# A two-layer decoder: layer two's negated row maxima as bf16 parts, one unread product per sequence, and newly written queues

## The chip, the cores and the metric

The kernel is written for one Trainium2 chip and runs on one of its cores. Its engines work side by side, each down its own queue: TensorE (PE), VectorE (DVE), ScalarE (ACT), GpSimd (POOL) and SyncE (SP, which here only issues DMAs). They wait for each other on semaphores. The metric is device time in microseconds, the median of several executions; lower is better.

## The reference, cut to what matters

Sixteen sequences of 128 tokens with width 128 pass through two layers, every step fp32 and followed by a layer norm of x plus the step:

```python
# layer 1
x = ln(x + attention_with_relative_positions(x))      # 16 heads of 8
x = ln(x + cross_attention(x, ctx))                   # 16 heads of 64, 77 keys
x = ln(x + moe(x))                                    # 7 experts and a no-op, top 2, capacity 256
# layer 2
x = ln(x + ln_affine(x + linear_attention(x)))        # 16 heads, rank 16, decay and gate
x = ln(x + cross_attention(x, ctx))                   # 16 heads of 8, 77 keys
x = ln(x + bit_linear(silu(conv3(bit_linear(x)))))    # int8 activations, ternary weights
```

In layer two's cross attention, softmax needs each row's maximum over its 77 keys. The kernel forms exp(k q - max) with the keys on the partitions, so the maxima have to reach the products' accumulators transposed.

## The kernel before, in words

One tile is one sequence (128 tokens on the partitions, or width on the partitions after a transposition). Layer one is software-pipelined over the sequences t: prefix `a_` is self attention, `b_` cross attention, `rel*` the relative scores, `keys`, `v0` the context's projections, `r_*` the router's work in four batches of sequences (0 to 7, 8 to 12, 13 and 14, 15), `r_send` the scatter of tokens to expert slots. After all sixteen come the experts' products (`m_*`), and then layer two, again pipelined: `c_` gathers and norms the experts' output, `d_` is the linear attention, `e_` the cross attention, `f_` the convolutional feed-forward.

Each engine's queue is written out by hand. `ORDER1` and `ORDER2` hold one list of names per engine. `rounds` (L162) repeats the list for i = -8, -7, ...; an entry `name:s` emits that step for t = i + s. `TAIL1` ends layer one with entries `name:t`, skipping what has been emitted already; `UNTIL1` says where it takes over. An engine never passes over a step, so a step that waits holds all that is listed behind it on its engine. Below, `b_lg:14` is step b_lg for t = 14.

One round of layer two, by the steps that matter here. DVE masks the four groups of linear attention scores (d_m0 to d_m3, L1679), bounds f's exponential (f_clamp, L1771), does f_silu and f's quantization (f_q0 to f_q4, L1721 to L1752), sums and norms c, d (d_add, d_st, d_ag, d_n0, d_n1, D_st, D_ag, d_norm) and e (e_div L1323, e_add, e_st, e_ag, e_norm), turns the rotary products (d_r0, d_r1 L1657, d_rope L1663), quantizes f's input (f_i0 to f_i4), norms f's output (f_norm L1348), forms d's queries and keys (d_q L1667, d_k L1673), and takes e's four maxima (e_m0 to e_m3, L1363).

PE runs d_rank (L882, products of the rotary result), f_x (a transposition, L978), e_s (e's scores, which need ACT's copy qe of e_q), f_up (one bf16 and three fp32 products of 512 columns: six records), e_nm, d_s01 (the first three groups of d's scores), e_st (e's scores again, keys on the partitions), d_s3, e_inj, d_v, d_out, e_v. In e_nm, PE transposes the tile of negated maxima, ACT copies it to `nmT`, and e_inj (L714) adds row a of each 32-row strip (a from 0 to 3) to the accumulators of e_st: sixteen fp32 products with a selecting matrix `picksel`, four strips at once. Then ACT takes the exponentials e_e0 to e_e3. ACT also copies d_v's result to `xTr` (step d_v of its list, L1106), which d_out multiplies by the output weight; the sum d_add follows on DVE. In the trace an fp32 product makes two records, a bf16 one makes one. `idle(b, n)` issues n products of ones that nobody reads; before the change they stand at the start and end of layer two and near the end of layer one.

## Time and profile before

| | us |
|---|---|
| median of 3 runs (745.8 to 747.18) | 746.79 |
| the profiled execution | 751.72 |
| its span, first to last instruction | 749.9 |
| PE, DVE, ACT, POOL busy in the span | 664.9, 562.7, 420.0, 207.4 |

Layer one's rounds fill about 50 to 375, the routing's end and the experts 375 to 440, layer two's rounds the rest. Busy time says how much of a stretch an engine has instructions under way; which engine sets the pace of a stretch is read from who waits for whom. A name such as `k` or `bank` stands for several tiles, and buffer numbers are left out.

### The profile page before, as it was taken

How to read it: one execution, taken by the hardware profiler on the slowest of the kernel's cores; microseconds unless marked ns; L12 is line 12 of the kernel's file. 1: busy time of each engine (PE TensorE's matmuls, PEld its weight loads, DVE VectorE, ACT ScalarE, POOL GpSimd, SP SyncE). 2: the span in 40 equal slices, each digit the busy share in tenths (PEclk: the TensorE clock that was granted, in tenths of full speed). 3: DMA queues.
4: the chain of work that ended last, by engine and by line, in shares of the span. 5: the costliest groups of instructions: out<-in, count | busy, mean ns of one | idle time of the engine just before them, and what ended most of it. 6: DMA issues, size and time to landing. Idle time of an engine off the chain costs nothing.

```text
span 749.9 us, 20658 instructions
## 1 busy us (share of the span) xinstructions
PE 664.9 (89%) x7838; PEld 505.8 (67%) x7838; DVE 562.7 (75%) x2029; ACT 420.0 (56%) x1412; POOL 207.4 (28%) x213
## 2 busy tenths in 40 slices
PE   5877999999999999998878988999899989999896
PEld 2445677777777777776757976666666666666664
DVE  1246788888888999977656657888877888888853
ACT  3767777777777757763211224555555555555542
POOL 4411333333333335224434122222222222222100
PEclk9967999999999999999899999999999999999999
DMA  9775555555555435720122100000000001110000
GB/s 347 261 245 183 174 173 173 172 173 173 173 172 169 144 98 176 275 106 23 32 89 68 41 24 9 12 13 12 13 13 16 13 13 14 14 13 13 6 5 7
DMA packets 48257, 72.17 MB, mean 96 GB/s; under 512 B 2832, under 2 KB 43280, under 8 KB 45472
## 3 DMA queue, kind: packets, MB, share of 16 engines
q1 hardware_dynamic: 45120, 61.80, 24.4%
q0 software_dynamic: 2320, 5.18, 3.2%
q10 hardware_dynamic: 720, 3.88, 1.3%
q8 instruction: 63, 1.03, 0.6%
q14 instruction: 34, 0.28, 0.1%
HBM read 32.38 MB, written 38.47 MB: 94 GB/s over the span
## 4 chain that ended last, share of the span: by engine, by line
PE 49%; DVE 27%; ACT 12%; issue 8%; another core or an unknown queue 2%; DMA 2%; POOL 1%; SPq 0%; DVEq 0%; ACTq 0%
PE bank L562 40%; ACT sc L1072 4%; PE bank L623 4%; PE bank L710 3%; DVE k L1679 3%; DVE sc L1301 2%; DVE scol L1721 2%; ACT kbd L1221 1%; ACT kbd L1222 1%; ACT q L1111 1%; DVE k L1657 1%; DVE kbd L1771 1%; DVE nmxb L1370 1%; DMA xT_ld<-xT 1%
## 5 line engine op out<-in xcount | busy, mean ns | idle before, releaser
L1072 ACT ACTIVATE sc<-sc,nmxa 128x128 f32<-128x128 f32 x256 | 99.0, 391 | 37.2 <-DVE nmxa L1301 37.2
L501 POOL TENSOR_TENSOR early<-early,recb 128x616 f32<-128x616 f32 x32 | 38.9, 1216 | 179.5 <-DVE recb L1394 179.5
L1301 DVE CUSTOM_DVE_ANT_0 sc<-bank,rel 128x128 f32<-128x128 f32 x256 | 56.3, 286 | 14.7 <-PE bank L562 14.5
L1679 DVE TENSOR_TENSOR k<-bank,k_sb 128x512 f32<-128x512 f32 x64 | 41.1, 685 | 28.9 <-PE bank L562 22.2
L1072 ACT ACTIVATION_READ_ACCUMULATOR sc<-sc,nmxa 128x1 f32 x256 | 48.8, 191 | 0.0
L478 POOL TENSOR_TENSOR rext<-rext,ones 128x1008 f32<-128x1008 f32 x16 | 29.9, 1868 | 54.0 <-ACT rext L1050 53.9
L1050 ACT ACTIVATE rext<-bank 128x512 f32<-128x512 f32 x64 | 34.8, 610 | 17.6 <-PE bank L562 17.6
L623 PE MATMUL bank<-k_sb,sc 128*128 128x128 f32 x256 | 37.5, 294 | 7.3 <-issue 6.5
L562 PE MATMUL bank<-k,xdT 128*128 128x512 f32 x96 | 43.8, 592 | 0.0
L537 POOL TENSOR_TENSOR oTb<-x_all,row_sb 128x128 f32<-128x128 f32 x16 | 7.3, 458 | 131.8 <-DVE pTa L1700 131.8
L1311 DVE COPY pTa<-bank 128x512 f32<-128x512 f32 x32 | 21.2, 663 | 25.2 <-PE bank L623 25.2
L623 PEld LDWEIGHTS bank<-k_sb,sc 128*128 128x128 f32 x256 | 31.1, 151 | 11.9 <-issue 11.1
L562 PEld LDWEIGHTS bank<-xTb,wb 128*128 128x128 f32 x256 | 29.8, 191 | 12.5 <-issue 12.5
L510 POOL DMA_INDIRECT xg_dram<-x_all,to_slot x32 | 31.4, 980 | 24.7 <-DVE to_slot L1530 16.7
L527 POOL DMA_INDIRECT pTa<-yg_dram,of_slot x32 | 31.4, 980 | 24.6 <-DMA yg_dram<-sc 17.7
L1124 ACT ACTIVATE early<-early 128x308 f32<-128x308 f32 x64 | 27.5, 456 | 18.3 <-DVE early L1379 18.2
L562 PE MATMUL bank<-pTb,v 77*32 77x128 f32 x1024 | 33.9, 283 | 2.7 <-DVE early L1379 2.5
L562 PE MATMUL bank<-kbd 32*128 32x256 f32 x256 | 36.2, 400 | 0.1
L1116 ACT ACTIVATE pTb<-bank 77x512 f32<-77x512 f32 x64 | 34.2, 586 | 3.4 <-PE bank L562 3.4
L562 PE MATMUL bank<-k_sb,ones 128*128 128x256 f32 x144 | 36.0, 399 | 0.0
L562 PE MATMUL bank<-k,q 64*128 64x77 f32 x512 | 32.5, 276 | 2.2 <-ACT q L1111 1.6
L562 PEld LDWEIGHTS bank<-k,q 64*128 64x128 f32 x512 | 30.0, 187 | 6.4 <-ACT q L1111 5.9
(278 smaller groups left out, 1854.8 us busy)
## 6 DMA issues: line engine op xcount, KB each, us to landing
rel_dram<-rext SPq DMA_DIRECT2D x16, 2040.0 KB, 7.4
rel<-rel_dram SPq DMA_DIRECT2D x16, 960.0 KB
rext<-w_up SPq DMA_DIRECT2D x1, 1792.0 KB, 9.0
rel<-w_down SPq DMA_DIRECT2D x1, 1792.0 KB, 7.2
wb<-w_b ACTq DMA_DIRECT2D x1, 1604.0 KB, 16.4
xT_ld<-xT SPq DMA_DIRECT2D x16, 64.0 KB, 7.6
x_all<-x ACTq DMA_DIRECT2D x1, 1024.0 KB, 11.7
rel<-rel_dram SPq DMA_DIRECT2D x16, 64.0 KB
```

Source lines behind the costliest of these rows:

```text
L478: G.tensor_tensor(rext[:, :, 0:MAX_REL - 1], rext[:, :, MAX_REL - 1:MAX_REL].broadcast_to(shape), ones[:, 0:1].unsqueeze(2).broadcast_to(s ...
L501: G.tensor_tensor(pB[:, part, :], pB[:, part, :], recb[:, part].unsqueeze(2).broadcast_to([P, 8, C]), ALU.mult).then_inc(b_even, 1)
L510: G.indirect_dma_start(out=xg_dram, out_offset=bass.IndirectOffsetOnAxis(ap=to_slot[:, 2 * t + k:2 * t + k + 1], axis=0), in_=x_all[:, t, ...
L527: G.indirect_dma_start(out=g[k][t % 3], out_offset=None, in_=yg_dram if t else yg_dram[0:(E + 1) * P], in_offset=bass.IndirectOffsetOnAxis ...
L562: return pe.matmul(out_, lhsT, rhs, start=start, stop=stop)
L623: last = pe.transpose(bank[i][:, a * P:(a + 1) * P], sc[:, 4 * i + a, :], ident)
L1050: A.activation(rext[:, 4 * i:4 * i + 4, MAX_REL - 1:MAX_REL - 1 + P], bank[i][:].rearrange("p (a r) -> p a r", a=4), ACT.Copy).then_inc(r_ ...
L1072: last = A.activation(sc[:, h, :], sc[:, h, :], ACT.Exp, bias=nmxa[:, h:h + 1], scale=-1.0, accum_out=suma[:, h:h + 1])
L1116: A.activation(dst[0:C, 4 * i:4 * i + 4, :], bank[b][0:C, :].rearrange("p (a i) -> p a i", a=4), ACT.Exp).then_inc(exped["b"], 1)
L1124: A.activation(part, part, ACT.Exp).then_inc(exped["b"], 1)
L1301: last = V.tensor_tensor_reduce(out=sc[:, h, :], in0=bank[i][:, a * P:(a + 1) * P], in1=rel[:, t % 2, h, :], scale=-1.0, scalar=FAR, op0=A ...
L1679: V.tensor_tensor(scd[:, 4 * i:4 * i + 4, :], bank[(1, 2, 0, 1)[i]][:].rearrange("p (a t) -> p a t", a=4), const("causal").unsqueeze(1).br ...
```

## The change

- ORDER1, TAIL1 and ORDER2 are written anew for all engines. Every step of before is still issued as often for every t.
- e_m0 to e_m3 write to a small tile `nmx`. A new step `e_sp` (e_split, four DVE instructions) writes them into `nme` as three bf16 parts per value, 12 columns of each strip. It stands between d_q and d_k.
- e_nm is a bf16 product with a bf16 identity instead of an fp32 transposition. e_inj's sixteen products are bf16; the selecting matrix picks three rows, so that the parts are added up.
- d_out issues one product `idle(0, 1)` (fp32, 256 columns) before it waits for its operand.
- bias_parts, during the experts' products, makes the two bf16 tables `identb` and `pickb`.
- In the list of SP f_store is written with another shift, which gives the same sequence of stores.

```diff
@@ -72,84 +72,53 @@
 
 
 ORDER1 = {
-    "pe": ("a_t2:1 a_t3:1 b_t1:-1 b_t2:-1 b_t3:-1 a_s:2 keys:2 b_q a_v:1 b_s0 b_s1 a_qkv:4 b_v0:-1 b_v1:-1 "
-            "a_out:1 b_out:-1 rel_last:4 b_r:-2 v0 b_lg:-2 rel:4 b_x:1 a_t0:2 a_t1:2 r_rank:-3 b_t0").split(),
-    "dve": ("a_rec a_t3 b_t1:-2 b_t3:-2 a_m0:1 b_qhi:-1 a_m1:1 b_m0:-1 b_m1:-1 b_l0:-1 b_m2:-1 b_l1:-1 b_l2:-1 a_div "
-            "b_norm:-3 b_u0:-2 b_m3:-1 b_u1:-2 a_qkv:3 b_l3:-1 b_sum0:-1 a_add b_rec0:-1 a_st rel_last:3 "
-            "b_add:-2 a_ag b_sum1:-1 a_ln r_p1:-4 r_n:-5 b_lg:-3 r_w:-19 r_a:-3 r_b:-4 b_st:-2 r_s:-3 r_p0:-3 "
-            "b_rec1:-1 b_ag:-2 v0:-1 a_t1:1 r_rows:-4 r_c:-4").split(),
-    "act": ("a_e0:4 b_qlo:2 a_e1:4 a_e2:4 a_v:3 a_qkv:6 b_e0:2 keys:4 b_e1:2 a_e3:4 b_e2:2 b_e3:2 b_r a_ln:3 "
-            "v0:2 r_a rel0:6 rel1:6 b_x:3 rel2:6 rel3:6 a_t0:4 b_ln:1 b_t0:2 a_t2:4 b_t2:2").split(),
+    "pe": ("b_t2:-1 b_t3:-1 a_s:2 b_q a_v:1 b_s0 b_s1 a_qkv:4 b_v0:-1 b_v1:-1 a_out:1 b_out:-1 rel_last:4 b_r:-2 v0 "
+            "b_lg:-2 rel:4 b_x:1 r_rank:-3 a_t0:2 b_t0 a_t1:2 keys:3 a_t2:2 a_t3:2 b_t1").split(),
+    "dve": ("r_c:-5 a_t1 a_t3 b_t1:-2 b_t3:-2 a_m0:1 a_m1:1 b_qhi:-1 b_m0:-1 b_m1:-1 b_l0:-1 b_m2:-1 b_l1:-1 r_w:-22 "
+            "b_l2:-1 b_m3:-1 a_div b_u0:-2 b_norm:-3 b_u1:-2 a_qkv:3 b_l3:-1 b_sum0:-1 a_add r_p1:-4 b_rec0:-1 a_st "
+            "rel_last:3 a_ag b_sum1:-1 a_ln b_lg:-3 r_b:-4 r_n:-4 r_a:-3 a_rec:1 b_add:-2 r_s:-3 r_p0:-3 b_rec1:-1 "
+            "b_st:-2 b_ag:-2 v0:-1 r_rows:-4").split(),
+    "act": ("a_e1:4 b_e0:2 a_v:3 a_qkv:6 b_e1:2 a_e2:4 a_e3:4 b_e2:2 b_e3:2 b_r a_ln:3 v0:2 r_a keys:4 rel0:6 b_x:3 "
+            "rel1:6 rel2:6 rel3:6 a_t0:4 b_ln:1 a_t2:4 b_t0:2 b_t2:2 a_e0:5 b_qlo:3").split(),
     "pool": "b_n0:1 b_n1:1 r_send:-9 rel_fill:5".split(),
-    "sp": "load_rel:5 store_rel:6".split(),
+    "sp": "store_rel:5 load_rel:5".split(),
 }
 
 UNTIL1 = 14
 TAIL1 = {
...
-            "r_c:12 r_w:12 b_norm:14 b_u0:15 b_u1:15 b_lg:14 a_ag:12 r_a:14 b_st:9 b_add:15 r_n:12 b_sum1:10 "
-            "r_c:7 b_st:15 b_ag:15 b_l3:11 r_c:6 b_norm:15 r_s:14 a_m0:14 r_p0:14 b_m1:11 b_sum1:11 b_lg:15 "
-            "r_p1:14 r_a:15 r_s:15 r_b:14 r_p0:15 r_p1:15 r_s:10 r_n:14 r_b:15 r_rows:14 r_c:14 b_sum1:12 "
...
+    "pe": ("b_t2:13 b_t3:13 b_q:14 r_rank:13 b_s0:14 b_s1:14 a_v:15 b_v0:13 b_v1:13 b_r:12 a_out:15 b_out:13 b_lg:12 "
+            "v0:14 b_x:15 b_t0:14 b_t1:14 b_t2:14 b_t3:14 b_q:15 r_rank:11 b_s0:15 b_s1:15 b_v0:14 b_v1:14 b_r:13 "
+            "b_out:14 v0:15 b_lg:13 b_t0:15 b_t1:15 b_t2:15 b_t3:15 r_rank:12 b_v0:15 b_r:14 b_v1:15 b_out:15 b_lg:14 "
+            "b_r:15 b_lg:15 r_rank:14 r_rank:15").split(),
+    "dve": ("r_w:8 r_rows:13 r_w:9 r_n:13 r_p1:13 a_t1:14 r_c:11 r_b:13 b_norm:11 r_a:13 a_t3:14 r_p1:10 b_t1:12 "
+            "r_w:7 r_n:11 r_rows:11 r_s:13 r_p0:13 b_t3:12 a_m0:15 a_m1:15 b_qhi:13 r_b:10 r_p0:11 b_m0:13 b_m1:13 "
+            "b_l0:13 r_n:10 b_m2:13 b_l1:13 b_l2:13 a_div:14 b_u0:12 r_n:15 b_m3:13 b_u1:12 b_l3:13 b_sum0:13 "
+            "a_add:14 b_rec0:13 a_st:14 r_c:9 a_ag:14 b_sum1:13 a_rec:15 a_ln:14 b_add:12 b_rec1:13 b_st:12 b_ag:12 "
+            "r_w:13 b_lg:11 v0:13 b_t1:13 b_norm:12 b_t3:13 a_t1:15 a_t3:15 b_qhi:14 b_m0:14 r_rows:10 b_m1:14 "
+            "b_l0:14 b_m2:14 b_l1:14 b_l2:14 b_m3:14 a_div:15 b_l3:14 b_u0:13 b_u1:13 a_add:15 b_sum0:14 a_st:15 "
+            "b_rec0:14 a_ag:15 b_sum1:14 b_add:13 b_lg:12 b_st:13 a_ln:15 r_a:12 b_rec1:14 v0:14 b_ag:13 r_s:12 "
+            "b_t1:14 b_t3:14 r_c:13 r_p0:12 b_qhi:15 r_p1:11 r_p1:12 b_m0:15 b_norm:13 b_m1:15 b_l0:15 b_l1:15 "
+            "b_m2:15 r_s:11 r_b:12 b_l2:15 b_m3:15 b_l3:15 r_w:10 b_u0:14 b_u1:14 b_sum0:15 b_rec0:15 b_sum1:15 "
+            "b_add:14 b_st:14 b_rec1:15 b_ag:14 v0:15 b_norm:14 b_lg:13 b_t1:15 b_t3:15 r_rows:12 r_c:12 b_u0:15 "
+            "b_u1:15 b_add:15 r_b:11 b_lg:14 r_n:12 r_w:12 b_st:15 r_a:14 b_ag:15 r_s:14 b_norm:15 b_lg:15 r_a:15 "
+            "r_s:15 r_p0:14 r_p1:14 r_b:14 r_p0:15 r_p1:15 r_w:11 r_b:15 r_rows:14 r_c:14 r_w:14 r_n:14 r_w:6 "
+            "r_rows:15 r_a:11 r_c:10 r_c:15 r_w:15").split(),
+    "act": "b_r:14 r_a:14 b_ln:15 b_r:15 r_a:15".split(),
+    "pool": ("r_send:5 r_send:6 b_n0:15 b_n1:15 r_send:7 r_send:8 r_send:9 r_send:10 r_send:11 r_send:12 r_send:13 "
+            "r_send:14 r_send:15").split(),
+    "sp": ("").split(),
 }
 ORDER2 = {
-    "pe": ("v1 f_turn:-2 e_out:-1 d_qk:1 e_x d_gv:1 f_down:-2 e_q d_rank:1 f_x:-1 e_s f_up:-1 e_nm d_s01:1 "
-            "e_st d_s3:1 e_inj d_v:1 d_out:1 e_v d_x:2").split(),
-    "dve": ("f_clamp:-1 d_m2:1 d_m3:1 f_silu:-1 c_s0:2 f_q0:-1 c_s1:2 c_st:2 c_ag:2 f_q1:-1 d_add:1 f_q2:-1 "
-            "d_st:1 d_ag:1 c_norm:2 f_q3:-1 f_q4:-1 d_n0:1 d_n1:1 D_st:1 D_ag:1 e_div v1:1 d_norm:1 e_add e_st "
-            "e_ag d_r1:2 e_norm d_r0:2 f_i0 d_rope:2 f_i1 f_add:-1 f_i2 f_st:-1 f_i3 f_ag:-1 f_i4 f_norm:-1 "
-            "d_gate:2 d_q:2 e_m0:1 e_m1:1 e_m2:1 e_m3:1 d_k:2 d_m0:2 d_m1:2").split(),
-    "act": ("e_e2 d_v:1 e_e3 c_ln:2 d_ln:1 e_v d_x:2 d_ln2:1 f_turn:-1 e_ln e_x:1 d_gates:2 e_q:1 f_ln:-1 f_x "
-            "d_sig:2 e_nm:1 f_exp f_sig e_e0:1 e_e1:1").split(),
-    "pool": "gather:2 e_res d_res:2 d_fade:2".split(),
-    "sp": "f_store:2".split(),
+    "pe": ("d_qk:1 e_x d_gv:1 e_q f_down:-2 e_s d_rank:1 f_x:-1 f_up:-1 e_nm d_s01:1 e_st d_s3:1 e_inj d_v:1 d_out:1 "
+            "e_v f_turn:-1 d_x:2 v1:1 e_out").split(),
+    "dve": ("d_m2:1 d_m3:1 c_s0:2 f_silu:-1 c_s1:2 f_q0:-1 c_st:2 d_add:1 c_ag:2 f_q1:-1 d_st:1 f_q2:-1 d_ag:1 "
+            "f_q3:-1 c_norm:2 d_n0:1 d_n1:1 D_st:1 e_div D_ag:1 f_norm:-2 v1:1 d_norm:1 e_add e_st f_q4:-1 e_ag "
+            "d_r0:2 d_r1:2 e_norm d_rope:2 f_i0 f_i1 f_add:-1 f_i2 f_st:-1 f_i3 f_ag:-1 f_i4 d_gate:2 e_m0:1 e_m2:1 "
+            "e_m3:1 e_m1:1 d_q:2 e_sp:1 d_k:2 d_m0:2 f_clamp d_m1:2").split(),
+    "act": ("e_e2 d_v:1 e_e3 c_ln:2 d_ln:1 e_v d_x:2 d_ln2:1 f_turn:-1 e_x:1 e_ln e_q:1 d_gates:2 f_x d_sig:2 f_ln:-1 "
+            "f_exp e_nm:1 f_sig e_e0:1 e_e1:1").split(),
+    "pool": "d_fade d_res:1 gather:2 e_res".split(),
+    "sp": "f_store:5".split(),
 }
 
 
@@ -246,8 +214,12 @@
-        nmb = sb("nmb", [P, P])
-        nmT = sb("nmT", [P, P])
+        nmx = sb("nmx", [P, 16])
+        nmr = sb("nmr", [P, 16])
+        nme = sb("nme", [P, P], BF16)
+        nmTe = sb("nmTe", [P, P], BF16)
+        identb = sb("identb", [P, P], BF16)
+        pickb = sb("pickb", [P, 4 * C], BF16)
@@ -462,7 +433,7 @@
-            G.memset(nmb[:], 0.0).then_inc(pre_pool, 1)
+            G.memset(nme[:], 0.0).then_inc(pre_pool, 1)
@@ -715,7 +686,7 @@
                 for a in range(4):
                     for i in range(4):
-                        last = mm(ps[i][0:C, a * P:(a + 1) * P], picksel[strip(i), a, :], nmT[strip(i), :],
+                        last = mm(ps[i][0:C, a * P:(a + 1) * P], pickb[strip(i), a * C:(a + 1) * C], nmTe[strip(i), :],
                                   start=False, stop=(a == 3))
                         if a == 3:
@@ -919,6 +890,7 @@
             def d_out(t):
+                idle(0, 1)
                 pe.wait_ge(oT_ready["d"], t + 1)
@@ -942,8 +914,8 @@
             def e_nm(t):
-                pe.wait_ge(maxed["b"], 4 * (B + t) + 4)
-                pe.transpose(bank[6][:, 3 * P:4 * P], nme[:], ident).then_inc(nm_ps, 1)
+                pe.wait_ge(maxed["b"], 4 * B + t + 1)
+                mm(bank[6][:, 3 * P:4 * P], nme[:], identb[:]).then_inc(nm_ps, 1)
 
@@ -1360,9 +1332,21 @@
                 def f(t):
                     dve.wait_ge(scores["b"], 4 * (base + t) + i + 1)
-                    V.tensor_reduce(nmb[:, 32 * i:32 * i + 4], bank[b][:, 0:4 * C].rearrange("p (a j) -> p a j", a=4),
-                                    AX.X, ALU.max, negate=True).then_inc(maxed["b"], 1)
-                return f
+                    keep(f"e_m{i}", t, V.tensor_reduce(
+                        nmx[:, 4 * i:4 * i + 4], bank[b][:, 0:4 * C].rearrange("p (a j) -> p a j", a=4),
+                        AX.X, ALU.max, negate=True))
+                return f
+
+            def e_split(t):
+                by_strip = nmx[:].rearrange("p (i a) -> p i a", a=4)
+                left = nmr[:].rearrange("p (i a) -> p i a", a=4)
+                parts = [nme[:].rearrange("p (i x) -> p i x", x=32)[:, :, 4 * k:4 * k + 4] for k in range(3)]
+                after(max(done[f"e_m{i}", t] for i in range(4)))
+                need(dve, nm_ps, t)
+                step(V.tensor_copy(parts[0], by_strip))
+                V.tensor_tensor(left, by_strip, parts[0], ALU.subtract)
+                step(V.tensor_tensor(parts[1], by_strip, parts[0], ALU.subtract))
+                V.tensor_tensor(parts[2], left, parts[1], ALU.subtract).then_inc(maxed["b"], 1)
 
             def b_max(i):
@@ -1628,6 +1612,8 @@
+                step(V.tensor_copy(identb[:], ident))
+                step(V.tensor_copy(pickb[:], const("picksel")))
@@ -1802,7 +1788,7 @@
-                **{f"e_m{i}": row_max(i, 3 + i, B) for i in range(4)}, "e_div": divide("e", 3, rbe, oTe), "e_add": e_out,
+                **{f"e_m{i}": row_max(i, 3 + i, B) for i in range(4)}, "e_sp": e_split, "e_div": divide("e", 3, rbe, oTe), "e_add": e_out,
@@ -1829,7 +1815,7 @@
-        "picksel": np.repeat(p % 32 == np.arange(4), C, axis=1),
+        "picksel": np.repeat((p % 32 < 12) & (p % 4 == np.arange(4)), C, axis=1),
```

## Rows read from the trace of the kernel before

**Rows 1.** Windows: us, each engine's busy time (instructions), granted clock, DMA share, GB/s.

```profile
200.00:300.00 100.00, 94.82 (x1156) 74.55 (x1156) 90.87 (x367) 73.08 (x272) 34.18 (x24) 1.00 0.49 164
...
440.00:450.00 10.00, 8.08 (x66) 5.78 (x62) 7.12 (x20) 2.21 (x9) 2.70 (x5) 0.83 0.05 13
...
500.00:600.00 100.00, 90.17 (x1249) 66.34 (x1250) 81.81 (x270) 54.72 (x169) 24.05 (x36) 1.00 0.06 13
```

**Rows 2.** Chain that ended last, second layer: start, us, what.

```profile
636.03 1.27 DVE k L1679 x2
...
649.10 3.63 PE bank L562 x15
...
653.96 1.27 DVE k L1679 x2
```

**Rows 3.** Timeline of PE, second layer: start, us, instruction, idle before and releaser.

```profile
637.73 1.03 PE L562 MATMUL bank<-nmT,k_sb 32*77 32x128 f32 x20
...
638.89 1.08 PE L562 MATMUL bank<-k,va 128*32 128x128 f32 x32
...
640.62 0.49 PE L562 MATMUL bank<-wl,xTr 128*128 128x128 f32 x2 [0.66 <-ACT xTr L1106]
...
644.29 0.49 PE L562 MATMUL bank<-wl,qa 128*128 128x128 f32 x2 [0.32 <-DVE qa L1323]
...
646.29 0.39 PE L562 MATMUL bank<-k,oTb 128*128 128x128 bf16 x4
...
647.61 1.16 PE L562 MATMUL bank<-k,wl 128*128 128x128 f32 x8 [0.59 <-DVE k L1663]
...
649.03 0.80 PE L562 MATMUL bank<-k,qa 32*128 32x308 f32 x8
...
649.77 0.39 PE L562 MATMUL bank<-cbrow,onesrow 128*128 128x512 bf16 x1
```

**Rows 4.** Timeline of DVE, the same round.

```profile
636.01 1.29 DVE L1679 TENSOR_TENSOR k<-bank,k_sb 128x512 f32<-128x512 f32 x2 [1.75 <-PE bank L562]
...
637.22 0.42 DVE L1771 TENSOR_SCALAR kbd<-kbd 128x512 f32<-128x512 f32 x1
...
641.30 0.28 DVE L1342 TENSOR_TENSOR y_d<-bank,oTb 128x128 f32<-128x128 f32 x1
...
644.66 0.35 DVE L1700 TENSOR_SCALAR pTa<-y_d,mv_D,rstd_D 128x128 f32<-128x128 f32 x1 [0.23 <-ACT rstd_D L1100]
...
646.36 0.35 DVE L1348 TENSOR_SCALAR x<-y_e,mv_e,rstd_e 128x128 f32<-128x128 f32 x1 [0.22 <-ACT rstd_e L1100]
...
649.16 0.35 DVE L1348 TENSOR_SCALAR out_sb<-y_f,mv_f,rstd_f 128x128 f32<-128x128 f32 x1 [0.44 <-ACT rstd_f L1100]
...
650.23 1.63 DVE L1363 TENSOR_REDUCE nmb<-bank 128x4 f32<-128x308 f32 x4
```

**Rows 5.** Timeline of ACT, the same round.

```profile
647.16 0.38 ACT L1213 ACTIVATE qa<-bank,col_sb 128x128 f32<-128x128 f32 x1
```

**Rows 6.** Timeline of PE, first layer, at a_t0.

```profile
232.46 1.12 PE L623 MATMUL bank<-k_sb,sc 128*128 128x128 f32 x8 [0.52 <-issue]
```

**Rows 7.** Timeline of DVE, small operations of the routing (to_slot:14).

```profile
391.42 0.16 DVE L1529 TENSOR_TENSOR r_u<-slot,r_u 128x4 f32<-128x4 f32 x1
...
391.62 0.17 DVE L1530 TENSOR_TENSOR to_slot<-r_u,k_sb 128x4 uint32<-128x4 f32 x1
```

**Rows 8.** Timelines of PE and of ACT, last sequence: ones behind f_up.

```profile
739.23 4.05 PE L562 MATMUL bank<-k_sb,ones 128*128 128x256 f32 x18
...
739.43 0.60 ACT L1217 ACTIVATE kbd<-bank 128x512 f32<-128x512 f32 x1 [3.06 <-PE bank L562]
```

**Rows 9.** Timelines, end of the first layer: PE's ones; DVE's router reads.

```profile
377.42 2.40 PE L562 MATMUL bank<-k_sb,ones 128*128 128x256 f32 x10
...
379.69 0.17 DVE L1418 TENSOR_TENSOR lg<-bank,row_sb 128x8 f32<-128x8 f32 x1 [6.48 <-remote]
...
384.77 0.17 DVE L1418 TENSOR_TENSOR lg<-bank,row_sb 128x8 f32<-128x8 f32 x1 [0.87 <-PE bank L562]
```

More of the change, by code:

```diff
@@ L225, in decoder @@
         ident = const("ident")
-        picksel = const("picksel").rearrange("p (a j) -> p a j", a=4)
         x_all = sb("x_all", [P, B, P])
@@ L318, in decoder @@
         ve, vd = va[0:2], va[2]
-        nme, nmTe = nmb, nmT
         xE, xD = x1[0:2], [pTa[:, 6 + i, :] for i in range(2)]
```

7 lines of the change are left out of this document (removed), and 42 rows, old and new, of the table TAIL1.

## The prediction

> **What bounds the kernel now.** I read the table of windows first, to split the span. The first layer's rounds (one sequence each) keep PE busy 94.8 of 100 us; the second layer's keep PE busy 90.2 and DVE 81.8 of 100 us, at granted clock 1.00 [rows 1]. Then the chain of waits: in the second layer it repeats every 17.93 us (653.96 - 636.03), so one round can be worked out and multiplied [rows 2]. Then the timelines of PE, DVE and ACT over that round [rows 3 to 5]. The reader is to see in them that the round is a relay. From 636.01 DVE runs almost without a gap through the masks (d_m), the gated feed-forward, four layer norms and the rotary sum (d_rope), which releases d_rank on PE at 647.61. Then PE is the runner for 6.4 us: d_rank, f_x, e_s, f_up (the 3.63 us stretch), e_nm and d_s01, until DVE gets its first mask input at 653.96. Inside this PE leg DVE idles 1.75 us, inside the DVE leg PE idles 0.66, 0.32 and 0.59 us. So work taken from either leg shortens the round; work put where the other engine leads is free up to its lead.
>
> In the first layer PE alone is the bound. Its one long gap per round is 0.52 us before a_t0, which waits until ACT has copied the first relative scores [rows 6].
>
> **The injection as bf16 parts.** e_inj is sixteen products on four row strips; the profile shows 32 records, two for each fp32 product, the last 20 in 1.03 us [rows 3]. Packed groups of 32 records take 1.08 us, 0.27 of it the length of one product, so 26 ns a record and 0.85 us for 32. Four bf16 products of 128x128 took 0.39 us together, four fp32 ones (eight records) 1.16: bf16 streams in about a quarter of the time. That makes 0.2 us for the sixteen if streaming sets it, 0.43 if each record keeps its 26 ns. Bounds: 0 (the pairs keep today's pace) to 0.65 us less. e_nm as a bf16 product saves 0 to 0.14 us of its 0.27. I take 0.6 and 0.1. It is partly covered: d_v behind it waits for the fourth mask, which needs d_s3, not e_inj. What it frees is ACT, whose first e_e exponential can start 0.6 us earlier, if its sigmoid is ready too (next part). Alone, this edit would be worth at most the 0.1 us of e_nm.
>
> **e_sp.** Four DVE instructions on 16 columns. None stands in the trace; dependent small operations in the routing start 0.20 us apart and last 0.17 [rows 7]. Two waits among the four: 0.20 + 0.10 + 0.20 + 0.17 = 0.67 us, bounds 0.5 and 1.0. Queued behind it are d_k and the masks; d_s01 and e_nm wait for it. It stands in DVE's 1.75 us lead, and f_norm (0.35 us with 0.44 us of idle before it [rows 4]) leaves that very stretch, where it saves 0.70 us on DVE. The two cancel; so e_sp costs nothing as long as f_up ends later, and 0.7 us a round if that cover went.
> The Trainium skill, "VectorE: DVE Perf Modes", section on the TRN2 errata, gives an SBUF operation 58 cycles plus its elements at 0.96 GHz. By that the four would take an estimated 0.3 us. The routing rows show 0.17 us each and a pitch of 0.20, so they decide.
>
> **The unread product in d_out.** One fp32 product of 256 columns: two records; 18 such records took 4.05 us, 0.21 us a piece without the last one's tail [rows 8], so 0.43 us. It falls into the 0.66 us [rows 3] that PE waits for ACT's copy of d_v's result. Cost 0, at most 0.1 when that copy comes earlier. With the cover gone: 0.43.
>
> **The new order, second layer.** Worked along one round, in this trace's times (old -> new):
> - f_clamp moves in front of d_m1, one mask of 0.60 us earlier (637.22 -> 636.6). ACT's sigmoid and exponentials follow it; with e_inj done by about 638.0 they start 0.6 us earlier. ACT's copy of d_v's product then waits only for PE (d_v ends at 639.97): d_out 640.62 -> 640.3, and e_v behind it as much.
> - d_add stands right behind c_st, and no dependent pair of statistics is adjacent any more; each such pair waits some 0.1 us. d_add 641.30 -> 640.85. e_out 644.29 -> 643.8. f_norm now fills most of the 0.23 us before d_norm: 644.66 -> 644.4.
> - Both rotary products now stand ahead of e_norm, in its 0.22 us wait, and f_i0 (0.19) behind d_rope. d_rope ends 0.8 us earlier, at 646.75.
> - On ACT e_q goes ahead of d_gates: qe, now 647.16 to 647.54, is done at 646.65. So e_s (0.74 us until the next product starts, 649.03 to 649.77) runs inside PE's 0.59 us wait instead of between f_x and f_up. d_rank: 647.61 -> 647.4, since it now waits for e_s and not for d_rope.
> - f_x follows at 648.3, ACT's copy takes until 648.95, and f_up starts at 649.0; it was 649.77. That is -0.77, and PE sits idle for the 0.4 us of the copy that e_s used to fill.
> - DVE meanwhile: the int8 steps and d_gate to 648.4; the four maxima (1.54 us from 648.35; they started at 650.23); d_q 0.6; e_sp 0.7; d_k ends at 651.5. f_up ends at 651.8. So PE stays the later one, by 0.3 us, and the loss of DVE's lead costs nothing. This is the thinnest margin of the sum.
> - POOL's gather and e_res move ahead of d_fade: five instructions are done by about 648.8, d_fade's input comes at 649.8; the gathered rows are used a round later. SP's store order is the same sequence. Both 0.
> With e_nm 0.1 us shorter a round becomes 0.8 us shorter by this working. Every meeting of two engines was taken as exact, so I take 0.7; bounds 0.2 and 0.9. Some 14 full rounds: -9.8 us. First and last rounds follow other waits: 0.
>
> **The new order, first layer.** The steady rounds keep a_t0 behind rel0, and that wait stays; PE's work is the same, and what moves on DVE and ACT (a_rec into the gap ahead of a_t1, b_t0 between a_t0 and a_t1) was not what PE waited for. 0, bounds -2 and +2. In the tail b_add:15 stood behind the wait for b_lg:14, which lasted to 379.69 [rows 9]; now it stands ahead of it, and b_r:14 runs a value product earlier. That brings the last router product, read at 384.77, 1 to 3 us forward. Against it, r_p0:14 (six small steps, 1.2 us) now comes after b_lg:15 instead of beside its wait, and r_n:14 (0.3) leaves the path. What they lead to is to_slot:14 (391.62), which starts the last sends. Sum -1.5, bounds -3 and +1.5.
>
> **Set-up.** Two conversions to bf16 (128 and 308 columns) on DVE amid the experts' products: 0.6 us by the maxima's 0.39 us per 308 columns, bounds 0 and 0.8; I take +0.4.
>
> Sum: -9.8 - 1.5 + 0.4 = -10.9 us on the profiled execution of 751.72. That one is 4.9 above the median of 746.79; off the median it is 735.9, and I say 736.0.
>
> **Rivals.**
> A. Little is left of the relay's gain: e_sp takes 1 us, or the packed bf16 pairs are no faster. The Trainium skill, "TensorE: Matmul & The Clock Gate", section "Back-to-back issue gap", has some 81 ns for each load and product of 128 columns. Sixteen in series would be an estimated 1.3 us, longer than now; the packed rows here, 26 ns a record, speak against series. As a mechanism of this kernel: pairs at 52 ns, as now, make e_inj as long as today, e_v keeps its start, and the round loses only what DVE saves at e_norm and f_norm, 0.1 to 0.4 us. 14 x -0.25 - 1.1 = -4.6: 742.
> B. The other side: the unread product delays the signal of the product ahead of it. At the end of layer one ten records of ones (377.42 to 379.82) stand behind the router product, and its reader on DVE starts only at 379.69, some 2 us late [rows 9]. If d_v's reader, ACT's copy, came even 1.5 us late each round, d_out and d_add, and all behind them, lose 1.5: (1.5 - 0.7) x 14 = +11: 757. It decides from 0.7 us on. Against it: 18 such records behind the last f_up from 739.23, and its reader started at 739.43, at once [rows 8]; one fp32 product is 0.43 us of cover, not 2.
> C. PE's clock falls. At 440 to 450, with PE busy 8.1 of 10 us, it was granted 0.83 [rows 1]. New gaps of 0.4 us (behind f_x) and 0.5 (ahead of d_v) come in each round. At the lower level the 3 us of f_up alone cost 3 us more: one such spell in four rounds cancels the gain, one in two gives about +10: 757. Against it: PE's share rises, as the round shrinks by as much as PE's work (17.93 less the three idles is 16.4 us now; less 0.7, plus 0.43, it is 16.1 of 17.2 after).
> D. The reordering of the first layer goes wrong in its start or steady rounds, 0.2 us a round or more, and layer two gives a third: 748.
>
> **How the numbers follow.** Forecast 0.61 (730 to 740), A 0.20, B 0.06, C 0.05, D 0.08. A measurement of this kernel tells 0.2% (1.5 us) from no change. A is nearly all faster; D is half no change, half slower, and some of A and of the forecast's working may end at no change. Faster 0.79, same 0.07, slower 0.14. Range 729.5 to 747.5: both bounds of the round (14 x 0.9 + 3 below; 14 x 0.2 less 1.5 the other way) and A; B, C and half of D are outside.
>
> **What would show it.** The period of the chain of waits in the second layer near 17.2 us. e_s ahead of d_rank, without PE idle between; f_up about 13.0 us after the first mask instead of 13.8. PE, not DVE, released last ahead of d_s01; if e_nm waits for nme, e_sp is the new wait. Two-record ones ahead of d_out, with less than 0.3 us idle around them. First-layer period 19.1 us unchanged. Wrong if the period stays above 17.7, if the clock in 500 to 600 is below 0.97, or if the first layer ends more than 3 us off.

## The result, and the profile after

| | before | changed |
|---|---|---|
| median of 5 runs each, us | 747.17 (745.80 to 747.99) | 742.02 (739.93 to 743.31) |
| span of the profiled execution | 749.9 | 740.2 |

The ratio is 0.9953, with a 95% interval of 0.993 to 0.9976: faster by 5.1 us, where 10.9 were forecast. Measured once more later, in 12 executions, it was 1.001 (0.9976 to 1.0045). So there are two questions: why the first measurement gave half of the forecast, and why the second gave nothing.

The two profiled spans differ by more than the medians do, because in the profile of before DVE waited 3.60 us for nmxb at the end of layer one, released by what the profile calls "remote", which it does not in this one. So layer two is read by its period, which no such wait touches.

Windows of the changed kernel, with the columns of [rows 1]:

```profile
200.00:300.00 100.00, 95.59 (x1166) 75.97 (x1163) 91.74 (x369) 72.87 (x271) 34.33 (x25) 1.00 0.50 164
440.00:450.00 10.00, 5.78 (x44) 4.20 (x40) 7.05 (x24) 4.13 (x15) 3.95 (x6) 1.00 0.05 13
500.00:600.00 100.00, 88.67 (x1267) 65.28 (x1273) 87.08 (x296) 57.39 (x174) 20.72 (x31) 1.00 0.06 12
```

The clock in layer two is 1.00 as in [rows 1]. PE's share went down and not up (90.2 to 88.7; 89.6 in a second trace of the same kernel); DVE's rose from 81.8 to 87.1. The first masks of three rounds, on the timeline of DVE:

```profile
610.53 0.69 DVE L1665 TENSOR_TENSOR k<-bank,k_sb 128x512 f32<-128x512 f32 x1 [1.60 <-PE bank L533]
...
628.22 0.69 DVE L1665 TENSOR_TENSOR k<-bank,k_sb 128x512 f32<-128x512 f32 x1 [1.60 <-PE bank L533]
...
645.89 0.69 DVE L1665 TENSOR_TENSOR k<-bank,k_sb 128x512 f32<-128x512 f32 x1 [1.60 <-PE bank L533]
```

A round takes 17.66 to 17.69 us (two of twelve 17.93), against 17.93 in [rows 2]. That is 0.26 us of the 0.7 forecast, and 14 x 0.26 = 3.6 of the 5.1 us. The rest is in layer two as well: the steady period leaves out three rounds of before that took 18.2 to 18.7 us, and the last round (17.93, now 17.25). From the first mask of the third sequence to that of the sixteenth, thirteen rounds, the trace of before takes 234.8 us and the changed one 229.9, 4.9 us less. PE in that round, the answer to [rows 3]:

```profile
631.09 1.08 PE L533 MATMUL bank<-k,va 128*32 128x128 f32 x32 [0.78 <-DVE k L1665]
632.10 0.70 PE L533 MATMUL bank<-k_sb,ones 128*128 128x256 f32 x2
632.64 0.42 PE L533 MATMUL bank<-wl,xTr 128*128 128x128 f32 x2
...
638.91 0.80 PE L533 MATMUL bank<-k,qa 32*128 32x308 f32 x8 [0.23 <-ACT qa L1185]
639.64 1.16 PE L533 MATMUL bank<-k,wl 128*128 128x128 f32 x8
641.08 0.33 PE L950 MATMUL bank<-k_sb,oTb 128*128 128x128 f32 x1 [0.29 <-DVE oTb L1726]
642.01 2.74 PE L533 MATMUL bank<-k,xdT 128*128 128x512 f32 x6 [0.60 <-ACT xdT L1078]
```

The reader is to take the times from the first mask at 628.22. The unread product (x2 of ones) runs straight on into d_out, without idle time. e_s starts at 10.7 us and d_rank at 11.4, as forecast. But f_x starts at 12.9 instead of 12.3, and what it waits for is f_i4 (L1726). f_up's first record, the bf16 one, is missing from this trace; in a second trace of the same kernel it starts at 13.6 and the wait before it is 0.37 us, not 0.60. DVE and POOL around f_i4:

```profile
638.38 0.35 DVE L1320 TENSOR_SCALAR x<-y_e,mv_e,rstd_e 128x128 f32<-128x128 f32 x1
640.00 0.50 DVE L1722 TENSOR_SCALAR oTb<-x,scol 128x128 f32<-128x128 f32 x1
640.53 0.50 DVE L1726 TENSOR_SCALAR oTb<-oTb,scol 128x128 f32<-128x128 f32 x1
```

```profile
638.21 0.99 POOL L498 DMA_INDIRECT pTa<-yg_dram,of_slot  x1 [0.15 <-issue]
639.50 0.95 POOL L498 DMA_INDIRECT pTa<-yg_dram,of_slot  x1 [0.30 <-issue]
640.47 0.47 POOL L514 TENSOR_TENSOR oTb<-pTa,row_sb 128x128 f32<-128x128 f32 x1
```

f_i3 and f_i4 take 0.50 us each. In the profile of before they took 0.27 and 0.29 on average, and POOL's gather started 3.1 us after the start of f_i4. Now f_i3 ends 0.05 us after the gather's second issue (640.45), and f_i4 0.09 us after e_res (640.94).

The last round of this same trace has no gather, and its e_res is done at 691.5, before f_i3. There both are quick, and the round takes 17.25 us instead of 17.67:

```profile
681.23 0.69 DVE L1665 TENSOR_TENSOR k<-bank,k_sb 128x512 f32<-128x512 f32 x1 [1.60 <-PE bank L533]
...
693.02 0.27 DVE L1722 TENSOR_SCALAR oTb<-x,scol 128x128 f32<-128x128 f32 x1
693.32 0.29 DVE L1726 TENSOR_SCALAR oTb<-oTb,scol 128x128 f32<-128x128 f32 x1
...
698.48 0.69 DVE L1665 TENSOR_TENSOR k<-bank,k_sb 128x512 f32<-128x512 f32 x1 [1.60 <-PE bank L533]
```

### The profile page after: what moved, and what is told of

Read it like the earlier page. It is cut to its first block, busy times and chain, and to the rows that moved or that the text cites. A ratio compares the mean times of both kernels' runs of the same rounds, so it can differ in the third digit from the quotient of the medians.

```text
span 740.2 us, 20275 instructions
## 1 busy us (share of the span) xinstructions
PE 652.3 (88%) x7598; PEld 497.2 (67%) x7614; DVE 572.5 (77%) x2095; ACT 420.2 (57%) x1412; POOL 206.9 (28%) x213
## 4 chain that ended last, share of the span: by engine, by line
PE 57%; DVE 24%; ACT 10%; issue 7%; DMA 1%; POOL 1%; SPq 0%; DVEq 0%; ACTq 0%
PE bank L533 48%; DVE k L1665 5%; ACT sc L1044 4%; PE bank L594 4%; PE bank L681 3%; DVE sc L1273 2%; DVE oTb L1726 1%; ACT q L1083 1%; DVE oTb L1722 1%; DVE nmxb L1354 1%; DVE kbd L1757 1%; DVE k L1643 1%; DMA xT_ld<-xT 1%; DVE k L1649 1%; DVE y_f L1744 1%
## 5 line engine op out<-in xcount | busy, mean ns | idle before, releaser
L533 PE MATMUL bank<-k_sb,ones 128*128 128x256 f32 x176 | 47.3, 407 | 0.0
L594 PE MATMUL bank<-k_sb,sc 128*128 128x128 f32 x256 | 35.7, 286 | 6.5 <-issue 5.7
L533 PEld LDWEIGHTS bank<-k_sb,ones 128*128 128x128 f32 x176 | 32.7, 199 | 8.7 <-issue 4.7
```

The lines of the kernel that those rows point to most:

```text
L533: return pe.matmul(out_, lhsT, rhs, start=start, stop=stop)
L594: last = pe.transpose(bank[i][:, a * P:(a + 1) * P], sc[:, 4 * i + a, :], ident)
```

## The experiments

Each kernel is compared with the kernel before on its own chip (747 to 751 us there). Where the clock moves, the period of layer two's rounds (from first mask to first mask, in the steady rounds) is the sharper reading: at full clock it repeats within some 0.02 us, but for one round in five or six that takes some 0.25 us longer, and up to 0.9 in the old order.

### Where the missing 0.4 us of a round went

**GpSimd's list undone** in the changed kernel:

```diff
-    "pool": "d_fade d_res:1 gather:2 e_res".split(),
+    "pool": "gather:2 e_res d_res:2 d_fade:2".split(),
```

> The changed kernel with GpSimd's list of layer two as it was: both groups of the gather and e_res behind d_fade and d_res. Theory 1 (the gather of two indirect DMA issues now runs beside DVE's f_i3 and f_i4, which take 0.50 us each instead of 0.27 and 0.29, with 0.18 us lost ahead of f_i3): both go back to 0.27 to 0.30 us, the round of layer two falls from 17.67 to 17.1 or 17.2 us, and the kernel takes 734 to 736 us, 0.989 to 0.992 of the changed kernel. Theory 2 (the missing gain lies in the path from f_x over ACT's copy to f_up, or in the first layer): 741 to 743 us, no change.

The round: 17.25 us. Its DVE:

```profile
648.16 0.27 DVE L1722 TENSOR_SCALAR oTb<-x,scol 128x128 f32<-128x128 f32 x1
...
648.47 0.29 DVE L1726 TENSOR_SCALAR oTb<-oTb,scol 128x128 f32<-128x128 f32 x1
```

From the first mask (636.38) f_x starts at 12.4 and f_up at 13.1 us. Theory 1 holds for the round. From the third sequence's first mask to the last one's, this trace takes 224.7 us, 5.2 less than that of the changed kernel. The total did not follow: 747.50, ratio to before 0.9919 (0.9883 to 0.9956). The profiled execution lost 5.8 us in layer two's first two rounds, by its clock (see below), and its first mask came at 442.5 us against 436.3. The saving shows in the totals of a later pair that differs by this list alone (the two kernels with unread products in the first round, below): 745.06 against 750.65 us.

**The new list alone in the kernel before** (the same two lines the other way round).

> The kernel before with GpSimd's list of layer two alone changed: the second group of d_res, the gather and e_res straight after d_fade. Theory 1: the gather now falls on f_i3 and f_i4 or on the writes just behind them wherever they meet, they grow by up to 0.2 us each, and 14 rounds cost 3 to 8 us: 750 to 755 us. If they do not meet here the kernel stays at 747 us, and the trace shows f_i3 and f_i4 at 0.27 and 0.29 us. Theory 2: 747 us whether they meet or not.

754.63 us, ratio 1.005 (1.0032 to 1.0068); the round 18.20 instead of 17.93, f_i4 0.50 us and f_i3 0.36 on average. As Theory 1 says, with the lower end of its price (3.6 us).

**e_res alone back behind d_fade.**

```diff
-    "pool": "d_fade d_res:1 gather:2 e_res".split(),
+    "pool": "d_fade e_res:-1 d_res:1 gather:2".split(),
```

> The changed kernel with e_res alone back behind d_fade on GpSimd; the gather stays ahead of it. Theory 1a (each DVE write that meets a GpSimd instruction is held until that instruction ends: f_i3 by the second issue of the gather, f_i4 by e_res): f_i4 back to 0.29 us, f_i3 still about 0.50 us with 0.18 us ahead of it, a round of 17.45 us, 3 us less in all than the changed kernel beside it. Theory 1b (the gather alone slows both): f_i4 stays at 0.50 us and the round at 17.67 us.

```profile
646.84 0.48 DVE L1722 TENSOR_SCALAR oTb<-x,scol 128x128 f32<-128x128 f32 x1
...
647.36 0.29 DVE L1726 TENSOR_SCALAR oTb<-oTb,scol 128x128 f32<-128x128 f32 x1
```

The round: 17.46 us. Theory 1a: the gather holds f_i3, e_res holds f_i4, each for some 0.21 us a round. In all 747.87, 0.9975 (0.9949 to 1.0002), beside 749.62 of the changed kernel, 1.8 us less; the two ratios' intervals overlap, so this reading rests on the round.

**Another form of f_i3 and f_i4**, beside the gather and away from it (with the list of the first experiment):

```diff
-  keep("f_i3", t, V.tensor_scalar(xd, xE[t % 2][:], scol[:, 2:3], ROUND, ALU.mult, ALU.add))
+  keep("f_i3", t, V.tensor_scalar(xd, xE[t % 2][:], scol[:, 2:3], rcol[:, 0:1], ALU.mult, ALU.add))
...
-  V.tensor_scalar(xd, xd, ROUND, scol[:, 1:2], ALU.subtract, ALU.mult).then_inc(f_xd, 1)
+  V.tensor_scalar(xd, xd, rcol[:, 0:1], scol[:, 1:2], ALU.subtract, ALU.mult).then_inc(f_xd, 1)
```

> The changed kernel with the rounding constant of f_i3 and f_i4 read from a column instead of being an immediate, so that both have two scalars per partition, the form of the layer norms' writes, which take 0.35 us beside the gather as well as away from it. Theory of the held port (only the faster form of the two, 0.27 us, is held by GpSimd): 0.35 us each under the same gather, nothing lost ahead of f_i3, a round of 17.3 to 17.4 us. Rival (anything on DVE that meets GpSimd's issue work is slowed, and the layer norms just miss it): 0.5 us or more each, a round of 17.67 us or above.

> The changed kernel with GpSimd's list as before and with the rounding constant from a column: shows how long f_i3 and f_i4 take in that form with no GpSimd beside them. If 0.35 us, then the slower form is held by the gather as much as the faster (0.49 and 0.50 us), and the held port of a faster form explains nothing. If 0.27 and 0.29 us, both forms run alike and the run beside the gather tells nothing on the form. A round of 17.2 to 17.4 us.

Beside the gather (748.73 us, ratio 1.0000, 0.9975 to 1.0026, round 17.69) first, then away from it (745.09 in one execution, round 17.36):

```profile
643.78 0.49 DVE L1724 TENSOR_SCALAR oTb<-x,scol,rcol 128x128 f32<-128x128 f32 x1
644.31 0.50 DVE L1728 TENSOR_SCALAR oTb<-oTb,rcol,scol 128x128 f32<-128x128 f32 x1
```

```profile
643.75 0.33 DVE L1724 TENSOR_SCALAR oTb<-x,scol,rcol 128x128 f32<-128x128 f32 x1
644.11 0.35 DVE L1728 TENSOR_SCALAR oTb<-oTb,rcol,scol 128x128 f32<-128x128 f32 x1
```

My theory that only the faster form is held falls: both forms end at 0.49 or 0.50 us there, because both end with GpSimd's instruction. The form away from the gather takes 0.33 and 0.35, so both are held for some 0.15 us until the other is done; their own work does not grow.

The Trainium skill, "SBUF — State Buffer", section "SBUF: two separate sides", says that GpSimd shares one pair of SBUF ports with those DVE instructions that run in a two-port mode or have two SBUF inputs, under an exclusive lock: the instruction that starts first keeps it for its whole duration, and the other one blocks. The traces agree for f_i3 and f_i4, which start second and end 0.03 to 0.09 us after GpSimd's instruction in four kernels. The write of e's norm at 638.38 above also starts second and is not held: it runs its usual 0.35 us inside the gather's first issue. No trace shows in which mode any of them ran. Whether the first issue differs from the second, or the early part of an issue from the late one, stays open.

### What each part is worth

**Order, parts and product apart.** The first kernel is the kernel before with the new lists (the diff is to these; GpSimd's of layer two stays as it was) and with `idle(0, 1)` in d_out; the second is the same without the product. Both have the maxima as in the kernel before, so e_sp is gone:

```diff
-                "e_m3:1 e_m1:1 d_q:2 e_sp:1 d_k:2 d_m0:2 f_clamp d_m1:2").split(),
+                "e_m3:1 e_m1:1 d_q:2 d_k:2 d_m0:2 f_clamp d_m1:2").split(),
```

> The changed order and the unread product with the maxima as they were (fp32, one transpose, no e_sp), and GpSimd's list of layer two as before. Against the kernel with the same order and the parts (17.24 us a round): DVE has 0.67 us less in the round and TensorE 0.7 us more. If the round is bound by TensorE's sum where the parts act, 17.6 to 17.9 us; if DVE's chain binds it, 17.0 to 17.2 us and the parts are worth nothing.

> The new order alone: maxima as in the kernel before (fp32), no unread product, GpSimd's list of layer two as before. With the product the same kernel takes 17.31 us a round. Theory (it is the bf16 parts that take the clock down, and the fp32 products of the maxima keep it up): the clock holds at 1.00 within layer two, the round stays 17.31 us, 743 to 749 us. Rival (the new order's own gaps take it down): rounds of 19 to 20 us among those of 17.3, 755 us or more.

With the product: 747.82, 0.9967 (0.9943 to 0.9992), round 17.31. Without: 743.38, 0.9897 (0.9853 to 0.994), round 17.31, and the clock holds:

```profile
500.00:600.00 100.00, 92.20 (x1335) 68.43 (x1337) 84.28 (x278) 58.18 (x176) 23.57 (x36) 1.00 0.07 13
600.00:680.00 80.00, 73.86 (x1042) 55.05 (x1032) 68.30 (x236) 46.56 (x146) 18.59 (x28) 1.00 0.09 13
```

So the order is worth 0.62 us a round and the parts 0.06 (17.31 to 17.25). That is neither end of what I expected of the first kernel: the new order binds on neither e_sp nor the maxima's products. In the trace of the changed kernel e_sp is done at 643.96, and e_nm starts at 644.58, right behind f_up: it does not wait for e_sp. The 4.4 us between the two totals are not the product's cost in a steady round, which is the same. The profile with the product has the clock at 0.54 from 448 to 466 us and first two rounds of 17.7 and 20.4 us, the one without 15.4 and 17.2; whether the product has a part in that no run tells.

**The three parts in the old order**: alone, and with the product.

```diff
-            "d_gate:2 d_q:2 e_m0:1 e_m1:1 e_m2:1 e_m3:1 d_k:2 d_m0:2 d_m1:2").split(),
+            "d_gate:2 d_q:2 e_m0:1 e_m1:1 e_m2:1 e_m3:1 e_sp:1 d_k:2 d_m0:2 d_m1:2").split(),
```

> The kernel before with the three bf16 parts alone (e_sp behind e_m3, all queues in the old order, no unread product). My prediction's terms for the parts are e_inj -0.6 us and e_nm -0.1 us on TensorE against +0.67 us of e_sp on DVE ahead of the injected maxima: a round of 17.9 us plus or minus 0.2, so 747 to 752 us beside 750 us, and the gain of the change lies in the order. If the parts themselves bring the gain, the round falls to 17.5 us or less.

> The kernel before with the three bf16 parts and the unread product, all queues in the old order. The parts alone cost 4% here, by a clock that fell to half in every round of layer two (20.5 us a round). Theory (the parts take TensorE work out just where it is thinnest, and the unread product stands in for it): the clock holds, a round is 17.8 to 18.1 us, 747 to 753 us. Rival (the old order with the parts has another gap that lets the clock fall, and the product does not mend it): 760 us or more.

Alone 784.08, ratio 1.0407 (1.036 to 1.0454), 20.5 us a round; with the product 751.44, 1.002 (0.9989 to 1.0052), 18.09 us. The same stretch of the two:

```profile
500.00:600.00 100.00, 90.27 (x1053) 70.53 (x1062) 76.56 (x263) 50.50 (x154) 20.00 (x30) 0.83 0.05 11
```

```profile
500.00:600.00 100.00, 89.50 (x1198) 63.38 (x1201) 84.93 (x285) 54.81 (x166) 23.17 (x34) 1.00 0.07 14
```

My expectation for the parts alone missed by over 30 us. It looked at engine time only. PE looks busier at 0.83 than at 1.00, because everything on it takes longer. In the slow rounds of the first kernel the clock falls behind two waits of PE, 0.78 us ahead of d_v and 0.65 us ahead of d_out; the first is not there with fp32 maxima [rows 3]. The theory of the second kernel holds, at the upper end of its range: against the product alone (next, 17.92) the parts cost 0.17 us a round in the old order.

**The product alone in the kernel before** (`+ idle(0, 1)` at the head of d_out).

> The kernel before with the unread product alone. Theory (the product lies in a wait of TensorE and only keeps up the clock, which layer two of the kernel before has at 1.00 anyway): a round of 17.93 us as before, 748 to 751 us. Rival B of my prediction (the product holds up d_v's signal): 1 us or more a round, 760 us.

750.95, 0.9999 (0.997 to 1.0027), round 17.92: free, and worth nothing there. Rival B of the prediction falls.

**e_s back between f_x and f_up** in the new order alone (PE's list), beside the new order alone once more:

```diff
-    "pe": ("d_qk:1 e_x d_gv:1 e_q f_down:-2 e_s d_rank:1 f_x:-1 f_up:-1 e_nm d_s01:1 e_st d_s3:1 e_inj d_v:1 d_out:1 "
+    "pe": ("d_qk:1 e_x d_gv:1 e_q f_down:-2 d_rank:1 f_x:-1 e_s f_up:-1 e_nm d_s01:1 e_st d_s3:1 e_inj d_v:1 d_out:1 "
```

> The new order alone (maxima in fp32, no unread product, GpSimd's list as before), with e_s back between f_x and f_up on TensorE. My prediction's largest step is that e_s (0.74 us) runs inside TensorE's wait ahead of d_rank in the new order, 0.4 us of which it gives back as a wait for the copy of f_x. If that holds, the round grows from 17.31 us by 0.2 to 0.4 us, 14 x 0.3 = 4 us more than the kernel run beside it. If the gain of the order comes from elsewhere (f_clamp, the layer norms' statistics, d_rope), the round stays at 17.3 us.

> The new order alone once more: maxima in fp32, no unread product, GpSimd's list as before, in more executions. A round of 17.31 us and the clock at 1.00 within layer two, 0.987 to 0.993 of the kernel before, which beats the changed kernel (0.995 and 1.001).

753.31 against 745.10 us; ratios 1.0049 (1.0018 to 1.0079) and 0.993 (0.9902 to 0.9958). The round goes from 17.31 to 17.60, as expected, which makes 4 us of the 8. The other 4 are a fall of the clock at layer two's start (17.5 and 19.1 us for the first two rounds, against 14.7 and 17.2), which neither theory foresaw.

```profile
634.99 0.80 PE L531 MATMUL bank<-k,qa 32*128 32x308 f32 x8
635.95 2.74 PE L531 MATMUL bank<-k,xdT 128*128 128x512 f32 x6 [0.16 <-issue]
```

Here e_s fills the copy's wait ahead of f_up (f_up's bf16 record is missing here too: the first fp32 one starts 0.96 us after e_s, where in [rows 3] the bf16 one starts after 0.74); in the new order it stands ahead of d_rank, and f_up waits 0.37 us.

### The clock

**The changed kernel without the unread product**, and the same with GpSimd's old list of layer two:

```diff
             def d_out(t):
-                idle(0, 1)
                 pe.wait_ge(oT_ready["d"], t + 1)
```

> The changed kernel without the unread product in front of d_out; the rest is the same. My theory, that the product of two instructions fills time in which TensorE waits or is ahead: 741 to 743 us, and the granted clock of layer two stays at 1.00. The rival that the product holds up the signal of d_v's eviction: 738 us or less. The rival that it keeps the clock up: 745 us or more with a clock below 1.00 in layer two.

> The changed kernel with the gather and e_res back behind d_fade and d_res, and without the unread product. If what keeps the clock is TensorE's busy share, which is higher in the round of 17.24 us than in that of 17.67 us, the clock falls less often than in the kernel without the unread product alone, and the time lies between 740 and 755 us against 747 to 751 us of the kernel before. If only the unread product's place in the round counts, the clock falls in as many rounds as there (5 or 6 of 15, 2.5 us each) and the time is about 760 us.

765.22, ratio 1.0189 (1.0151 to 1.0226): the rival that the product keeps the clock up holds. The second took 757.52, ratio 1.0047 (0.9998 to 1.0096); that ratio leans on one execution of 745.98 us, the other eleven took 755.9 to 762.4, and the medians give 1.0095. Its clock fell in fewer rounds, as the theory says, but it took longer than the 740 to 755 us expected: its first two rounds took 18.7 and 23.1 us. In the first kernel, rounds of 17.68 us stand beside four of 20.0 to 20.2:

```profile
515.00:520.00 5.00, 5.00 (x69) 3.18 (x68) 3.33 (x11) 1.68 (x5) 0.56 (x1) 1.00 0.01 3
520.00:525.00 5.00, 3.83 (x75) 3.05 (x76) 4.51 (x16) 3.65 (x10) 0.00 (x0) 0.76 0.02 3
525.00:530.00 5.00, 5.00 (x54) 4.52 (x47) 2.77 (x12) 1.74 (x6) 0.62 (x2) 0.56 0.04 13
530.00:535.00 5.00, 4.39 (x35) 3.17 (x34) 4.72 (x18) 2.94 (x12) 2.91 (x5) 1.00 0.14 26
```

And PE in the same place:

```profile
521.04 1.08 PE L533 MATMUL bank<-k,va 128*32 128x128 f32 x32 [0.78 <-DVE k L1664]
522.52 0.78 PE L533 MATMUL bank<-wl,xTr 128*128 128x128 f32 x2 [0.40 <-ACT xTr L1077]
523.23 1.94 PE L533 MATMUL bank<-pTb,va 77*32 77x128 f32 x32
```

After the two waits around d_v, which follow the quick bf16 e_inj, the clock falls from 2.4 to 1.2 GHz: the 32 records of e_v, which take 1.08 us in the changed kernel at full clock, take 1.94. With the product in the second wait the clock holds. With GpSimd's old list there was one such round among the steady ones (the others 17.24), so the place isn't all that counts; with fp32 maxima, whose e_inj takes twice the records, there was none, with the product or without.

**The changed kernel once more**, in 12 executions.

> The changed kernel as it is, on the chip of the three runs beside it. A round of layer two at full clock takes 17.67 us, as in its first profile; the ratio to the kernel before is 0.993 to 0.998. Theory of the clock (between two layers the clock falls in some executions and not in others, about 5 us each time): the executions spread over 5 us or more here too.

749.62 (745.62 to 756.80). Seven executions of clock 0.969 to 0.974 took 746 to 750 us, five of 0.957 to 0.961 took 752 to 757. The profiled one is of the second kind (clock 0.961): layer two's first round takes 18.3 us instead of 15.3, the next 19.5 instead of 17.0, 5.5 us in all; behind them the rounds are 17.68 as ever. That the other four executions of low clock fell at the same place is inferred from their mean clock; they have no trace.

```profile
444.00:448.00 4.00, 2.36 (x33) 1.57 (x26) 2.49 (x10) 1.48 (x6) 0.00 (x0) 1.00 0.00 0
448.00:466.00 18.00, 15.29 (x133) 11.66 (x133) 9.76 (x26) 5.25 (x15) 3.98 (x6) 0.53 0.03 8
466.00:470.00 4.00, 3.42 (x75) 2.87 (x74) 2.70 (x11) 2.17 (x9) 0.00 (x0) 0.98 0.01 4
```

In the first measurement no execution of the changed kernel had a clock below 0.970. But the fall is not the whole loss. The span of this profile is 10.2 us longer than that of the first (750.4 and 740.2). The first mask comes at 440.9 instead of 436.3 us, which is 4.6 of it, with four waits for "remote" at the end of layer one that the first trace does not have; the two first rounds are the other 5.5. And the seven executions of the higher clock have a median of 748.43, 2.0 us under that of before (750.39), not 5.

The fall at layer two's start is not the change's own either: it stands in the profiles of the new order alone with the product (17.7 and 20.4 us), of e_s back, and, smaller, in two kernels of the old order (16.7 and 18.0 with the product, 16.7 and 18.5 with GpSimd's new list).

**Unread products in the waits of that first round**, in the changed kernel and with GpSimd's old list:

```diff
             def d_x(t):
+                if t == 1:
+                    idle(7, 5)
...
             def e_x(t):
+                if t == 0:
+                    idle(7, 1)
...
             def e_scores(t):
+                if t == 0:
+                    idle(7, 1)
...
             def e_nm(t):
+                if t == 0:
+                    idle(7, 6)
```

> The changed kernel with unread products in the waits of TensorE in the first round of layer two: five ahead of d_x(1), one ahead of e_x(0), one ahead of e_s(0), six ahead of e_nm(0). Theory (in about half of its executions the changed kernel's clock falls to 0.50 in the waits of that round and stays there until the second round, 5.5 us): it no longer falls there, the first rounds take about 15.3 and 17.0 us in nearly every execution, the executions lie within 3 us of each other, and the median is 745 us or 0.990 to 0.994 of the kernel before. Rival (the fall has nothing to do with these waits): half of the executions are 5 us slower as before, ratio 0.998 to 1.001.

> The same unread products, with the gather and e_res back behind d_fade as well. If both losses are found, they add up: rounds of 17.24 us, no fall of the clock at the start of layer two, 738 to 741 us, 0.984 to 0.988 of the kernel before.

750.65, ratio 1.0003 (0.9977 to 1.003), and 745.06, 0.9913 (0.9886 to 0.994). In both profiles the first round is 15.9 us and the clock of 448 to 466 stays up, so the fill does what it is for, at 0.6 us, and no execution of either has a clock below 0.966. Yet the first kernel's ratio is the rival's: without the fall it is no faster than before (749.62 without the fill, 750.65 with it), and its executions still spread from 747 to 755. The totals are 4 to 6 us above what I expected. What is left lies ahead of layer two: its first mask came at 444.1 us here, and at 436.3 in the first profile of the changed kernel (440.4 in that of before).

The pair itself is clean: it differs by GpSimd's list alone, on one chip, with the clock of the first rounds up in both. 5.6 us lie between the medians, 5.3 us between the two traces, from the first sequence's first mask to the last one's (262.9 and 257.6).

**The first layer's lists of before** in the changed kernel (ORDER1, UNTIL1 and TAIL1).

> The changed kernel with the first layer's queues in the order of before; layer two as changed. My prediction gave the new order of the first layer 1.5 us, all in its tail: 743.5 us. If the whole gain measured (5 us) came from the first layer, 747 us. If the new order of the first layer costs time, 740 us or less.

748.02, 0.9946 (0.9919 to 0.9974), between the two values of the changed kernel, 0.9953 and 1.001. A gain of the new first layer can't be seen; a cost isn't excluded. The write of to_slot:14, to which the prediction's sum for the tail leads, came at 387.3 us in the first trace of the changed kernel and at 391.6 in that of before. But in the other thirteen traces with the new lists it came at 392.5 to 396.7, and in the six with the old ones at 388.1 to 393.7. Waits for "remote" stand ahead of it in every trace but that first one of the changed kernel.

## Why the prediction was wrong, step by step

**The step that failed** is "POOL's gather and e_res move ahead of d_fade ... Both 0." It asked whether POOL would be late, which it isn't, and not what its instructions do to DVE's while they run side by side. Measured: 17.67 - 17.25 = +0.42 us a round, in the twelve rounds that have it (not fourteen): 5.2 us between the traces of layer two, 5.6 between the medians of the clean pair. That is nearly all of the 5.8 us between forecast and result. A rival for it was missing. That A names 742, and 742.02 was measured, is luck: A's mechanism is refuted, since e_sp took the 0.67 us forecast and e_inj, from first record to last, 1.3 us instead of 2.0.

**The rest of the relay held.** Without that list the round is 17.25 us by the same order and the same parts; 17.23 was forecast (17.93 - 0.7). Over the thirteen rounds that is 10.1 us less than before, where the sum has 9.8 for layer two. f_x starts 12.4 us after the first mask (12.3 forecast) and f_up 13.1 (13.0). e_s inside the wait ahead of d_rank was measured at 0.29 us net, near the 0.34 of the working (0.74 less the 0.4 of the copy, which measures 0.37). The parts in this order are worth 0.06 us; the working, too, gave them no more than e_nm's 0.1.

**The unread product** costs nothing at full clock in three pairs of kernels (17.93 and 17.92, 17.31 and 17.31, 17.68 and 17.68). Rival B is refuted; the late reader that it was priced from had waited for "remote" by the trace. But "Cost 0" missed its worth: without it the changed kernel would be slower than the kernel before, by 1.9%.

**Rival C, the clock**, got 0.05. In the steady rounds it didn't come, thanks to that product. My reason against it (PE's share rises) was wrong: it fell from 90.2 to 88.7, and a share of busy time tells neither where the waits are nor how dense the products around them. At the start of layer two, which I priced at 0, it came in one profiled execution of the second measurement and, by their clocks, in four more of the twelve. It is about half of what that measurement lost; the rest lies ahead of layer two and stays open, as does why the median did not move once the first round was filled.

**The first layer** (-1.5) and the set-up (+0.4) were not resolved. In the first pair of traces to_slot:14 came 4.4 us earlier, in all later ones of the new lists later than in the first of before. Waits for "remote" in the tail came and went: 2.48, 3.16, 4.33 and 2.56 us in the second profile of the changed kernel, none in the first. What they are, no view tells. What is left between forecast and result, under 1 us, can't be placed.

**The range.** By its own terms it would run from 731.2 (746.8 - 12.6 - 3) to 745.5 (746.8 - 2.8 + 1.5); the prediction states 729.5 to 747.5, some 2 us more at either end.

**The simplest good version** is the new order alone: GpSimd's list of layer two as before, fp32 maxima, no product. 0.9897 (0.9853 to 0.994) in four executions and 0.993 (0.9902 to 0.9958) in six, against 0.9953 and 1.001 of the changed kernel. It can't be told apart from the changed kernel with GpSimd's old list, 0.9919 (0.9883 to 0.9956), and 0.9913 (0.9886 to 0.994) with the first round filled. But it has less in it, and the clock of its steady rounds holds by itself.
